# The normalisation of a graph layer: 28 chunks of 14 rows on 127 partitions in place of 30 chunks of 13 rows on 128

## What is computed

```python
ss, vv = xs[senders], xv[senders]            # projected features of each edge's sender
m0 = w[:, 0] * ss ...                        # weighted by a small MLP of the edge length, and its direction
msg_s = segment_sum(mid_s, receivers, 50000) # sum over edges by receiver
out = concat([msg_s @ W_out0, msg_v @ W_out1]) / (sqrt(64) * 16)
x = layernorm(x + out)                       # mean and variance over the 128 features, eps 1e-5
```

## Time and profile before

| | |
|---|---|
| time, median of 3 runs | 1347.6 us (1347.39 to 1348.72) |
| the profiled execution | one execution, span 1340.7 us from its first to its last instruction; so some 7 us of the median lie outside the span |
| busy: PE, DVE, ACT, POOL | 977.7, 688.6, 544.5, 1046.8 us |
| moved by DMA | 130.06 MB, mean 97 GB/s |
| loads of chunks by SP / stores by SP / stores by ACT | 30 / 29 / 1, of 832 KB each |
| granted TensorE clock, mean | 0.784 of full |

### The profile page before, as it was taken

One profiled execution on the slowest core, in us unless ns is written; L12 is line 12 of the kernel. 1 busy time (PEld: TensorE's weight loads), 2 busy tenths in 40 slices (PEclk: granted clock), 3 DMA queues, 4 the chain that ended last, 5 costly groups with the idle time before them and its releaser, 6 DMA issues.

```text
span 1340.7 us, 26289 instructions
## 1 busy us (share of the span) xinstructions
PE 977.7 (73%) x6206; PEld 919.7 (69%) x6206; DVE 688.6 (51%) x2880; ACT 544.5 (41%) x1403; POOL 1046.8 (78%) x923
## 2 busy tenths in 40 slices
PE   2896777786868868877876777887788778777810
PEld 1795777776767758767776777777777777677710
DVE  5762443466465465465366456366456556545402
ACT  5342232254344434444444435435435444424401
POOL 6547888888888888888888888888888888788771
PEclk9896877878787877887787878787778787878765
DMA  5778853343543443453443443444444444443332
GB/s 154 194 179 189 191 109 62 69 92 41 141 92 41 120 113 41 92 123 59 91 117 67 91 107 75 92 92 90 92 92 90 92 92 91 90 91 67 66 32 64
DMA packets 82531, 130.06 MB, mean 97 GB/s; under 512 B 16168, under 2 KB 66891, under 8 KB 81232
## 3 DMA queue, kind: packets, MB, share of 16 engines
q0 software_dynamic: 68992, 51.43, 28.2%
q1 hardware_dynamic: 12888, 77.14, 17.0%
q10 hardware_dynamic: 632, 1.29, 0.3%
HBM read 78.31 MB, written 77.09 MB: 116 GB/s over the span
## 4 chain that ended last, share of the span: by engine, by line
issue 37%; POOL 28%; DMA 27%; POOLq 6%; SPq 1%; DVE 0%; ACT 0%; ACTq 0%; DVEq 0%
DMA acc<-msg,index_now 17%; POOL sender L444 17%; DMA acc<-in_x_dram 9%; POOL acc L462 8%; POOLq L432 3%; POOL index_now L425 3%; POOLq L433 1%; SPq L297 1%; POOLq L434 0%; POOLq L458 0%; ACT normed L720 0%; DMA total<-acc 0%; POOLq L425 0%; POOLq L461 0%; POOLq L478 0%
## 5 line engine op out<-in xcount | busy, mean ns | idle before, releaser
L462 POOL DMA_INDIRECT acc<-msg,index_now x392 | 624.6, 1593 | 151.9 <-issue 124.9
L444 POOL DMA_INDIRECT sender<-in_x_dram,index_now x392 | 394.1, 1005 | 111.5 <-issue 99.9
L527 PE MATMUL ps_sT<-ident,sender 128*128 128x128 f32 x392 | 83.1, 349 | 269.1 <-DMA sender<-in_x_dram,index_now 268.9
L580 PE MATMUL ps_msg<-outw,sumT 128*128 128x64 f32 x1568 | 254.8, 334 | 0.0
L568 PEld LDWEIGHTS ps_sum<-same,mid 128*128 128x128 f32 x1568 | 248.1, 233 | 9.4 <-DVE mid L960 0.8
L580 PEld LDWEIGHTS ps_msg<-outw,sumT 128*128 128x128 f32 x1568 | 253.6, 253 | 0.0
L527 PEld LDWEIGHTS ps_sT<-ident,sender 128*128 128x128 f32 x392 | 54.7, 174 | 288.6 <-DMA sender<-in_x_dram,index_now 288.5
L568 PE MATMUL ps_sum<-same,mid 128*128 128x128 f32 x1568 | 250.9, 313 | 0.7 <-DVE mid L960 0.7
L938 DVE TENSOR_TENSOR proj<-ps_up,vec_all 128x384 f32<-128x384 f32 x98 | 54.3, 554 | 370.5 <-PE ps_up L548 361.1
L659 ACT COPY sumT<-ps_sum 128x512 f32<-128x512 f32 x196 | 114.9, 586 | 243.6 <-PE ps_sum L568 243.4
L720 ACT ACTIVATE normed<-total,shift,rstd 128x128 f32 x391 | 156.9, 481 | 50.6 <-DVE shift L1011 45.0
(11 more groups left out here) (140 smaller groups left out, 1089.1 us busy)
## 6 DMA issues: line engine op xcount, KB each, us to landing
acc<-in_x_dram SPq DMA_DIRECT2D x80, 312.5 KB
total<-acc SPq DMA_DIRECT2D x30, 832.0 KB
out_dram<-normed SPq DMA_DIRECT2D x29, 832.0 KB
sender<-in_x_dram,index_now POOLq DMA_INDIRECT x392
acc<-msg,index_now POOLq DMA_INDIRECT x392, 3.4
out_dram<-normed ACTq DMA_DIRECT2D x1, 832.0 KB
vec_raw<-in_edge_attr_dram SPq DMA_DIRECT2D x1, 576.0 KB
dst_raw<-in_dst_dram SPq DMA_DIRECT2D x1, 192.0 KB
```

Of the source, the lines that this page charges most:

```text
L444: pool.indirect_dma_start(sender[:, slot, i, :], None, x, bass.IndirectOffsetOnAxis(ap=index_now[:, b, 0, i:i + 1], axis=0)).then_inc(gath ...
L462: pool.indirect_dma_start(acc, bass.IndirectOffsetOnAxis(ap=index_now[:, b, 1, i:i + 1], axis=0), msg[:, msg_slot, i, :], None, compute_op ...
L527: mm = pe.transpose(ps_sT[:, P * i:P * (i + 1)], sender[:, k % RING, i, :], ident[:, :])
L580: mm = pe.matmul(ps_msg[:, i, 2 * MUL * h:2 * MUL * (h + 1)], sumT[:, b, i, h, :], outw[:, h, :], start=True, stop=True)
```

## The change

Rows are taken in 28 chunks of 14 rows on each of 127 partitions (1,778 rows), and 216 rows are left for the last piece, two rows on each of 108 partitions. The chunk count that the loops may reach is no longer one less than the number of chunks, but all of them; a second table (`done_half`) holds the index that the code behind the loops needs. Loads, stores, the moments and the normalisation use partitions 0 to 126.

```diff
-ROWS = 13
-CHUNK = P * ROWS
+ROWS = 14
+PARTS = 127
+CHUNK = PARTS * ROWS
 CHUNKS = N // CHUNK
 REST = N - CHUNKS * CHUNK
+REST_ROWS = 2
+REST_PARTS = REST // REST_ROWS
...
-                sp.dma_start(total[:, bass.ds(2 * (h % 2) + b, 1), :, :].rearrange("p b r d -> p (b r d)"),
-                             acc[bass.ds(N - CHUNK - c * CHUNK, CHUNK), :].rearrange("(p r) d -> p (r d)", p=P)
+                sp.dma_start(total[0:PARTS, bass.ds(2 * (h % 2) + b, 1), :, :].rearrange("p b r d -> p (b r d)"),
+                             acc[bass.ds(N - CHUNK - c * CHUNK, CHUNK), :].rearrange("(p r) d -> p (r d)", p=PARTS)
                              ).then_inc(total_in[b], 16)
...
-                sp.dma_start(out[bass.ds(N - CHUNK - c * CHUNK, CHUNK), :].rearrange("(p r) d -> p (r d)", p=P),
-                             normed[:, b, :, :].rearrange("p r d -> p (r d)")).then_inc(stored[b], 16)
+                sp.dma_start(out[bass.ds(N - CHUNK - c * CHUNK, CHUNK), :].rearrange("(p r) d -> p (r d)", p=PARTS),
+                             normed[0:PARTS, b, :, :].rearrange("p r d -> p (r d)")).then_inc(stored[b], 16)
...
-            done = sp.value_load(done_count[0:1, 0:1], min_val=0, max_val=CHUNKS - 1)
+            done = sp.value_load(done_count[0:1, 0:1], min_val=0, max_val=CHUNKS)
+            half = sp.value_load(done_half[0:1, 0:1], min_val=0, max_val=CHUNKS // 2 - 1)
             with sp.If(done % 2):
-                load(done // 2, 1)
-            with sp.If(CHUNKS - 1 - done):
+                load(half, 1)
+            with sp.If(CHUNKS // 2 - (done + 1) // 2):
...
-            sp.dma_start(total[0:REST, CHUNKS % 4, 0, :], acc[0:REST, :]).then_inc(total_in[0], 16)
+            sp.dma_start(total[0:REST_PARTS, CHUNKS % 4, 0:REST_ROWS, :].rearrange("p r d -> p (r d)"),
+                         acc[0:REST, :].rearrange("(p r) d -> p (r d)", p=REST_PARTS)).then_inc(total_in[0], 16)
...
-                link(dve.tensor_scalar(rising[:, :], rising[:, :], float(CHUNKS - 1), None, ALU.min))
+                link(dve.tensor_scalar(rising[:, :], rising[:, :], float(CHUNKS), None, ALU.min))
```

More of the change, by code:

```diff
@@ L61 @@
 assert UNITS % 2 == 0 and LAG % 2 == 0 and UNITS <= P and FULL == UNITS - 1 and FULL >= 96
-assert NORM_AFTER > STATS_AFTER and NORM_AFTER > RING // 2 and (UNITS - 2) % RING == 0 and CHUNKS % 2 == 0 and PIECES % 2 == 0 and N % PIECE == 0 and REST <= P
+assert NORM_AFTER > STATS_AFTER and NORM_AFTER > RING // 2 and (UNITS - 2) % RING == 0 and CHUNKS % 2 == 0 and PIECES % 2 == 0 and N % PIECE == 0 and REST == REST_ROWS * REST_PARTS and REST_PARTS <= P
 def bass_gnn(nc, x, src, dst, edge_vec, edge_len, W_up0, W_up1, w0, b0, w1, b1, w2, b2, W_out0, W_out1, out):
@@ L128, in bass_gnn @@
         done_count = sb("done_count", [1, 3], I32)
+        done_odd = sb("done_odd", [1, 3])
+        done_half = sb("done_half", [1, 3], I32)
         dst_all = sb("dst_all", [P, UNITS, G])
@@ L709, in _, with normalise @@
             act.sem_inc(normed_ready, 4)
-            def normalise(h, b, part, rows=ROWS, parts=P, store=False):
+            def normalise(h, b, part, rows=ROWS, parts=PARTS, store=False):
                 c = 2 * h + b
@@ L722, in normalise @@
                                         scale=rstd[0:parts, b, r:r + 1], bias=shift[0:parts, b, r:r + 1])
-                if part == 0 and rows > 1:
+                if part == 0:
                     return
@@ L728, in normalise @@
                 act.wait_ge(normed_ready, c + 5)
[L729 to L733, removed]
+                to = out[bass.ds(N - CHUNK - c * CHUNK, CHUNK) if rows == ROWS else slice(0, REST), :]
+                act.dma_start(to.rearrange("(p r) d -> p (r d)", p=parts),
+                              normed[0:parts, b, 0:rows, :].rearrange("p r d -> p (r d)")).then_inc(stored[b], 16)
             def pair(j, k):
@@ L756, in _ @@
             unit(UNITS, UNITS, tail=True)
-            done = act.value_load(done_count[0:1, 2:3], min_val=0, max_val=CHUNKS - 1)
+            done = act.value_load(done_count[0:1, 2:3], min_val=0, max_val=CHUNKS)
+            half = act.value_load(done_half[0:1, 2:3], min_val=0, max_val=CHUNKS // 2 - 1)
             with act.If(done % 2):
                 for part in range(2):
-                    normalise(done // 2, 1, part, store=True)
-            with act.If(CHUNKS - 1 - done):
+                    normalise(half, 1, part, store=True)
+            with act.If(CHUNKS // 2 - (done + 1) // 2):
                 with act.Fori((done + 1) // 2, CHUNKS // 2) as h:
@@ L765, in _ @@
                             normalise(h, b, part, store=True)
-            normalise(CHUNKS // 2, 0, 0, 1, REST, store=True)
+            for part in range(2):
+                normalise(CHUNKS // 2, 0, part, REST_ROWS, REST_PARTS, store=True)
         @block.vector
@@ L882, in make_dense_orders @@
                 for k, after in enumerate((0, STATS_AFTER, NORM_AFTER)):
-                    dve.tensor_copy(done_count[:, k:k + 1], final[:, PAIRS - after:PAIRS - after + 1])
+                    done = final[:, PAIRS - after:PAIRS - after + 1]
+                    dve.tensor_copy(done_count[:, k:k + 1], done)
+                    link(dve.tensor_scalar(done_odd[:, k:k + 1], done, float(CHUNKS - 1), None, ALU.min))
+                    dve.tensor_scalar(done_half[:, k:k + 1], done_odd[:, k:k + 1], -0.5, 0.5, ALU.add, ALU.mult)
                 link(dve.tensor_tensor(fresh[:, :], final[:, 1:1 + PAIRS], final[:, 0:PAIRS], ALU.subtract))
@@ L966, in unit, with moments @@
                     equal_receivers(u + 1, k + 1)
-            def moments(h, b, rows=ROWS, parts=P):
+            def moments(h, b, rows=ROWS, parts=PARTS):
                 c = 2 * h + b
@@ L975, in moments, with statistics @@
                 mm.then_inc(stats_ready, 1)
-            def statistics(h, b, rows=ROWS, parts=P):
+            def statistics(h, b, rows=ROWS, parts=PARTS):
                 c = 2 * h + b
@@ L1030, in _ @@
             pair(PAIRS - 1, UNITS - 2, last=True)
-            done = dve.value_load(done_count[0:1, 1:2], min_val=0, max_val=CHUNKS - 1)
+            done = dve.value_load(done_count[0:1, 1:2], min_val=0, max_val=CHUNKS)
+            half = dve.value_load(done_half[0:1, 1:2], min_val=0, max_val=CHUNKS // 2 - 1)
             with dve.If(done % 2):
-                moments(done // 2, 1)
-                statistics(done // 2, 1)
-            with dve.If(CHUNKS - 1 - done):
+                moments(half, 1)
+                statistics(half, 1)
+            with dve.If(CHUNKS // 2 - (done + 1) // 2):
                 with dve.Fori((done + 1) // 2, CHUNKS // 2) as h:
@@ L1039, in _ @@
                         statistics(h, b)
-            moments(CHUNKS // 2, 0, 1, REST)
-            statistics(CHUNKS // 2, 0, 1, REST)
+            moments(CHUNKS // 2, 0, REST_ROWS, REST_PARTS)
+            statistics(CHUNKS // 2, 0, REST_ROWS, REST_PARTS)
 _INS = ['x', 'src', 'dst', 'edge_attr_3', 'edge_weight', 'L0_gnn_W_up0', 'L0_gnn_W_up1', 'L0_gnn_mlp_w0',
```

## The result

The changed kernel takes **2378.9 us** (median of 4 runs, 2377.7 to 2381.5), against 1348.2 for the kernel before beside it: a ratio of 1.762, 95% interval 1.757 to 1.768. The forecast was 2530, range 2340 to 2830. The profiled execution has a span of 2376.0 us. A ratio is always to runs of the kernel before that were made beside those of the other kernel; their medians were 1344.6 to 1350.4. The 7 us that the sections above put outside the span are too many: wherever the record has both, the time is 1.4 to 2.2 us above the span (here 2377.7 and 2376.0), so the profiled execution of the kernel before, with its span of 1340.7, was most likely a shorter one than the three of its median.

A forecast was written before the change was run, and what follows sets the result against it. The prediction took POOL's gathers and scatters to bound the kernel before, and one DMA engine the changed one: 231 + 1954 + 320 + 15 = 2520 us, plus 7 outside the span, 2527, rounded to 2530; range 2340 to 2830.

The forecast's parts named there:

- The 7 us: Time outside the profiled span: median before 1347.6 against span 1340.7, so 7 us were added to the 2520 us sum.
- One DMA engine: Each chunk load or store of 127 pieces runs on one DMA engine instead of 16; chance 0.80 near its sum.
- equal shares: A transfer's pieces are dealt equally over engines, up to 16; 127 is prime, so one engine gets all 127.
- Price of a transfer: One chunk load or store of 910,336 bytes takes 34.9 us on one engine; 56 of them make 1954 us.
- the crowded mean: Upper price of a chunk transfer, from the mean of all transfers including waits beside others: 40.2 us, 2251 for 56.
- rival 1: Chunk transfers on one engine at the upper price, with q0's time on top: 2824 us; chance 0.10 for outside the range.
- what else this engine must do: The one engine's share of POOL's gathers and scatters from 231 us on: 320 us added, bounds nothing and 320.
- Before DVE stalls SP has issued the next load and the store of the chunk before: In the loop, SP's queue is not empty while DVE stalls, so the one engine runs without pause and sets the pace.
- Start and end: First load stays at 231 us; after the last chunk's load, 13 us of possible idle and 2 us for the store.
- What the profile would show: Signs: about 128 packets a transfer, DVE waiting over 1000 us, POOL about 40% busy, loads 70 to 85 us apart.
- Rival 2: Chunk transfers of 127 pieces use 16 engines with uneven shares; shorter end, 1337.6 us, 0.7% faster; chance 0.08.
- Rival 2's threshold: With k engines, a chunk's load and store take 70 / k of 35 us, q0 10: beat kept from k = 3.

The follow-up runs named there:

- experiments 1 and 2: 1: changed kernel, each load and store issued as 112 and 15 pieces, 1362.6 us; 2: kernel before, each issued as 127 and 1 pieces, 2388.1 us.
- Experiment 9: The changed kernel with the scatters of the first two of each unit's four tiles left out (196 of 392 gone): 2270.2 us.
- experiment 3: The changed kernel with only the loads split into 112 and 15 pieces, stores left at 127 pieces on one engine: 1691.9 us.
- experiment 5: The changed kernel with chunks still 1,778 rows apart, each transferred as 1,792 rows in 128 pieces, 14 rows done twice: 1338.3 us, ratio 0.9926 to the kernel before.

## Why the prediction was right, and where it was off

- **One DMA engine.** Right: 128 packets a transfer, and experiments 1 and 2 from both sides. The forecast rested on equal shares, which the trace of before had only for 1 piece and for multiples of 16. Now they are seen for others: 127 pieces on one engine, 124 on four, 122 on two, 15 on 15.
- **Price of a transfer, 34.9 us.** Right within the reading: 5.8% of 16 engines in 2098 us are 1947 us for 50.07 MB, 35.4 us per transfer. By the packet of a piece alone, 0.272 us for 7,168 bytes (the least and the median of the changed kernel's trace), it is 34.5. That a lone transfer does not pay the 40.2 us of the crowded mean was right, and rival 1 is out.
- **The mis-sized term: "what else this engine must do", 320 us.** The packet time itself was as forecast: 15.4% of 2098 us are 323 us. But it was not time that the engine was kept from the chunks. 55 transfers at 34.5 us are 1898 of the 2097 us of the stretch, so all else cost 199 us. 13 of these are pauses in the stream, which leaves 186 for POOL's packets, 134 less than the term. (The split rests on 34.5; with 35.4, which holds some waiting beside POOL's packets, 137 would be left.) Experiment 9 measures it directly: 0.47 us a scatter in place of 0.69. Together with the price (56 x 0.4, -22), the pauses (+13) and the start (-2) that makes -145, which is the difference between 2520 and 2376. The 7 us added on top of the span were 2. The bounds, nothing and 320, did hold the term.
- **"Before DVE stalls SP has issued the next load and the store of the chunk before, so the queue is not empty."** Right but for one pause of 12 us near the end, before the load of the last chunk, for which the table lets several pairs pass.
- **Start and end.** First load 229.1 (forecast 231); from the arrival of the last chunk to the end 49.9 us, of which 35 are the store: 15, as in the sum.
- **What the profile would show.** DVE's wait 1133.8 us (over 1000 forecast), POOL 44% busy (about 40%), loads 72 to 79 us apart (70 to 85), 128 packets a transfer, q1 24 GB/s (26). One sign was off by a factor of two: the mean DMA busy share from the first load on is 21%, 15.4 and 5.8 together, not a tenth or so. The prediction's own terms, 320 us of q0 on each engine and 1954 us on one, would have given 19% of some 2290 us.
- **Rival 2's number** was right where its condition holds: 1338.3 us measured in experiment 5, 1337.6 forecast. It is closer than its parts: the end was even shorter, 8.9 us in place of 11.1, and the last scatter came 5 us later. The spans of the two profiled executions differ by 6.4 us, the medians by 11.
- **Rival 2's threshold was wrong.** "The loop keeps its beat from k = 3 up" looked only at what an engine carries. With four engines the kernel takes 1581 us, with two 1683; three were not tried. The step that failed is that POOL's beat was treated as free of the transfer: a scatter beside a long one lands after 8 to 10 us in place of 3.4, and on four engines or fewer every transfer slows the loop while it lasts. It did not touch the forecast, since with one engine for both directions the stream of chunks is slower still.

The table has, for the kernel before with its transfers cut otherwise, how many engines carried the large part, for how long by the estimate of 0.253 us a piece (2.0 is from the earlier trace rows), and the kernel's time in us:

| pieces | engines | us per transfer, estimated | kernel |
|---|---|---|---|
| 128 | 16 | 2.0 | 1348 |
| 124 + 4 | 4 | 8 | 1581 |
| 122 + 6 | 2 | 15.4 | 1683 |
| 127 + 1 | 1 | 32 | 2388 |

With the small packets in between it is more: from the first to the last piece of a transfer the traces have 3.0, 10.9, 18.5 and 35.9 us in the median.

## What to carry to other kernels

Before a tile's partition count is changed, look at the factors of the new number: 127 for 128 leaves one DMA engine in sixteen, 124 leaves four, and a last piece that falls out better is not worth it. Keep the number of pieces at a multiple of 16, if need be by moving a few rows twice; that turned this change from 76% slower into 0.7% faster. And a transfer on few engines hurts long before those engines are full, because an indirect transfer that has pieces on them lands late (8 to 10 us here, in place of 3.4); count the landing time of those, not only the bytes.

## What the runs showed of the hardware that I had not expected

- SP's issue of a load lasts 0.35 us before and 35.5 us in the median in the changed kernel (the row of L338 in experiment 9): while the one engine had the transfer before it to do, the issue instruction itself did not end. With the queue empty, at 2285.27, it took 0.29. Whatever stands behind it in SP's stream waits too.
- Packets of another queue took 323 us of an engine's time by their durations and delayed a full stream by less than 199: durations of packets of two queues on one engine can't be added. A small piece between two long ones cost the stream 0.053 us (experiment 3).
- Cutting each of the 60 transfers into 64 and 64 pieces cost 4 us in all, into 112 and 16 pieces 21 us.
